# Experts of a routed feed-forward layer: the tile list walked in two halves instead of straight through

## The reference

```python
logits = flat @ router_weight.T + router_bias          # flat: layernorm(x), 4096 x 512
scores = jax.nn.softmax(logits, axis=-1)
topk_vals, topk_idx = jax.lax.top_k(scores, 2)
w = jnp.zeros((T, E)).at[arange(T)[:, None], topk_idx].set(topk_vals)
gu = jnp.einsum('th,ehf->tef', flat, gate_up_proj) + gate_up_bias
gate = jnp.minimum(gu[..., :I], 7.0)
up = jnp.clip(gu[..., I:], -7.0, 7.0)
act = (up + 1.0) * gate * jax.nn.sigmoid(gate * 1.702)
down = jnp.einsum('tei,eih->teh', act, down_proj) + down_bias
out = jnp.einsum('teh,te->th', down, w)
x = x + out
```

## Time and profile before

| | us |
|---|---|
| median of 3 runs | 1872.41 (1872.25 to 1873.85) |
| the profiled execution | 1873.76 |
| its span | 1872.0 |
| mean granted TensorE clock | 0.957 |
| attention and routing, up to the first gate-up matmul | 1130.5 |
| steps 1 to 36 of the expert stage | 671.5 |
| the last two steps and the end | 57.9 |

### The profile page before, as it was taken

The page is one execution under the profiler, slowest core; times in us unless marked ns, Lnnn a source line. Parts: engine busy times, 40 slices in busy tenths (PEclk is TensorE's granted clock), DMA queues, the critical chain, the costliest instruction groups (busy, mean ns, idle before and its releaser), DMA issues. The chain is left out here.

```text
span 1872.0 us, 31059 instructions
## 1 busy us (share of the span) xinstructions
PE 1692.8 (90%) x10405; PEld 1247.7 (67%) x10405; DVE 1334.0 (71%) x2330; ACT 691.5 (37%) x1317; POOL 469.3 (25%) x643
## 2 busy tenths in 40 slices
PE   4799999999999989999998729999999999999996
PEld 4555565555555555555554218998998989889895
DVE  4577667675766676767555587788888888888864
ACT  2254353443533533434334204242434433434221
POOL 3112112121121121121210202434343334233322
PEclk8999999999999999999998859999999999999998
DMA  5333233341332333413212142354544636636322
GB/s 185 86 91 112 85 90 86 94 113 52 112 104 61 100 106 103 112 53 102 75 57 79 46 145 74 106 201 127 191 142 176 218 111 218 212 120 221 96 75 79
DMA packets 104565, 216.04 MB, mean 115 GB/s; under 512 B 26704, under 2 KB 27728, under 8 KB 104400
## 3 DMA queue, kind: packets, MB, share of 16 engines
q1 hardware_dynamic: 77488, 135.53, 22.9%
q0 software_dynamic: 26912, 78.47, 13.3%
HBM read 204.19 MB, written 37.36 MB: 129 GB/s over the span
## 5 line engine op out<-in xcount | busy, mean ns | idle before, releaser
L595 DVE TENSOR_REDUCE negmax<-max_ps 128x2 f32<-128x1024 f32 x256 | 311.6, 1217 | 150.5 <-PE max_ps L376 148.9
L480 ACT ACTIVATE pt<-work 128x512 f32<-128x512 f32 x512 | 278.0, 597 | 327.4 <-PE work L388 325.5
L1188 PE MATMUL gu_ps<-xgT_hi,wg_hi 128*128 128x256 f32 x1248 | 354.8, 284 | 0.0
L1188 PE MATMUL gu_ps<-xgT_hi,wg_lo 128*128 128x256 f32 x1248 | 351.5, 282 | 0.0
L1188 PE MATMUL gu_ps<-xgT_lo,wg_hi 128*128 128x256 f32 x1248 | 351.4, 282 | 0.0
L376 PE MATMUL max_ps<-ks,qs 96*128 96x512 f32 x512 | 190.4, 454 | 56.9 <-DVE negmax L595 39.6
L1188 PEld LDWEIGHTS gu_ps<-xgT_hi,wg_hi 128*128 128x128 f32 x1248 | 235.3, 189 | 0.0
L1188 PEld LDWEIGHTS gu_ps<-xgT_lo,wg_hi 128*128 128x128 f32 x1248 | 235.3, 189 | 0.0
L1188 PEld LDWEIGHTS gu_ps<-xgT_hi,wg_lo 128*128 128x128 f32 x1248 | 235.2, 188 | 0.0
L376 PEld LDWEIGHTS max_ps<-ks,qs 96*128 96x128 f32 x512 | 85.2, 196 | 139.6 <-issue 74.1
L1248 ACT ACTIVATE sig<-gate 128x256 f32<-128x256 f32 x156 | 65.1, 417 | 304.2 <-DVE gate L1300 302.1
(11 more groups left out here) (192 smaller groups left out, 3078.6 us busy)
## 6 DMA issues: line engine op xcount, KB each, us to landing
raw_g<-w_gate_up SPq DMA_DIRECT2D x39, 2048.0 KB
raw_d<-w_down SPq DMA_DIRECT2D x39, 1024.0 KB
ks<-k_hi SPq DMA_DIRECT2D x256, 64.0 KB, 2.1
qs<-q_hi SPq DMA_DIRECT2D x256, 64.0 KB, 2.7
bd<-b_down SPq DMA_DIRECT2D x39, 256.0 KB
x_in<-x SPq DMA_DIRECT2D x8, 1024.0 KB, 5.8
ctxT_raw<-ctx_t SPq DMA_DIRECT2D x8, 1024.0 KB, 6.5
ks<-k_lo POOLq DMA_DIRECT2D x128, 64.0 KB, 2.3
```

Of the source, the lines that this page charges most:

```text
L480: e.activation(pt[k % 2][:, h, :], in_work("exp", u, k, h)[:, :], ACT.Exp, scale=scale).then_inc(exped.sem, 1)
L595: e.tensor_reduce(negmax[:, u % 2, n:n + 2], max_ps[:, :, :], AX.X, ALU.max, negate=True).then_inc(maxed.sem, 1)
L1188: ins = e.matmul(gu_ps[n % GU_BANKS][:, part, :], wg[s][pw][:, k, cols], xgT[s][px][:, k, :], start=(k == 0 and m == 0), stop=(k == KD - 1 ...
```

## The change

A function `in_list` turns a step number into a place of the list: step i takes place i // 2, plus 20 (half of 39, rounded up) for odd i. So even steps walk places 0 to 19 and odd steps places 20 to 38. Each read of the list by a step goes through it: the expert and the flag for a load, the flag for the conversions, the expert's column for the weights of the sum, and the row numbers. The flag of a place now compares it with the place directly before it, which is what its buffer held, and the flag of place 20, the first odd step's, is set to 1. The list itself is made as before.

```diff
+def in_list(i, n_tiles):
+    return i // 2 + i % 2 * ((n_tiles + 1) // 2)
...
-            then(e.memset(changed_f[:, 0:2], 1.0))
-            then(e.tensor_tensor(changed_f[:, 2:], expert_f[:, 2:], expert_f[:, :-2], ALU.not_equal))
+            then(e.memset(changed_f[:, 0:1], 1.0))
+            then(e.tensor_tensor(changed_f[:, 1:], expert_f[:, 1:], expert_f[:, :-1], ALU.not_equal))
+            last()
+            half = in_list(1, n_tiles)
+            then(e.memset(changed_f[:, half:half + 1], 1.0))
...
-    expert = e.value_load(tile_expert[0:1, tile:tile + 1], min_val=0, max_val=experts - 1)
-    changed = e.value_load(tile_changed[0:1, tile:tile + 1], min_val=0, max_val=1)
+    place = in_list(tile, tile_expert.shape[1])
+    expert = e.value_load(tile_expert[0:1, place:place + 1], min_val=0, max_val=experts - 1)
+    changed = e.value_load(tile_changed[0:1, place:place + 1], min_val=0, max_val=1)
...
         def changed_flag(e, i):
-            return e.to_reg(e.value_load(tile_changed[0:1, i:i + 1], min_val=0, max_val=1))
+            place = in_list(i, n_tiles)
+            return e.to_reg(e.value_load(tile_changed[0:1, place:place + 1], min_val=0, max_val=1))
...
-                e.tensor_tensor(w_all[:, :, :], xg[i % 2][:, :, D:DX], tile_hot[:, i, :, :], ALU.mult).then_inc(w_made.sem, 1)
+                e.tensor_tensor(w_all[:, :, :], xg[i % 2][:, :, D:DX], tile_hot[:, in_list(i, n_tiles), :, :], ALU.mult).then_inc(w_made.sem, 1)
...
-                e.tensor_copy(idx[i % IDX][:, :], token_of[:, i * SUB:(i + 1) * SUB]).then_inc(idx_made.sem, 1)
+                place = in_list(i, n_tiles)
+                e.tensor_copy(idx[i % IDX][:, :], token_of[:, place * SUB:(place + 1) * SUB]).then_inc(idx_made.sem, 1)
```

## The result

| | us |
|---|---|
| changed kernel, median | 1850.13 (1844.86 to 1853.42, 4 runs) |
| kernel before, beside it | 1872.33 (1869.89 to 1873.85, 4 runs) |
| ratio | 0.9872, 95% interval 0.9847 to 0.9897 |
| profiled execution and its span | 1853.42, 1851.7 |

Faster by 1.3%, as forecast in sign and inside the range; 3.4 us above the forecast of 1846.7. The profiled execution is 5.4 us above the span that was forecast for it, 1846.3. Where these lie can be read by comparing stages.

What follows compares the result with a forecast made beforehand. TensorE was taken as the bound, with 29.1 us of surplus in eleven steps where it waits for VectorE sums. Saving 25.2, plus 0.2 for routing, minus 0.7 at the end, gave a 25.7 us gain: 1846.7, range 1842.5 to 1856.

Steps and rivals of the forecast that it cites:

- The list read out of the conversions: Expert stage: tiles that change expert, read from weight conversion counts; 6 would change instead of 14, L1148's successor having 32 pieces.
- A quiet step of 17.85 us: Expert stage: a step without waits keeps 17.85 us; every step from 3 to 36 except 24, save tenths in 13 and 16.
- The pair: Neighbouring changing tiles 24 and 25: down and gate-up conversions meet in step 24, costing 2.7 us, bounds 0 and 4.6.
- The single changes: Five tiles changing expert without a changing neighbour: 0 us for steps 10, 23 and 33, at most 0.9 each.
- steps 13 and 16: Steps two behind a single change's down conversion: 0.3 us together from carried VectorE backlog, between 0 and 0.9 each.
- step 31: Kernel before, two steps behind a down conversion: its sum started 1.45 us later than step 11's, with 0.9 us surplus.
- Step 2: Start of the expert stage: its 0.9 us surplus belongs to tiles 0 and 1, which load in both orders, and stays.
- Routing: Where the flags are made: one more VectorE memset on the path, +0.2 us, bounds 0.1 and 0.6.
- The end: Last two sums, waiting for scattered rows to land: 0.7 us less with tile 36 full, bounds -0.7 and +2.
- Every change costs: Rival: each place of change costs 4.0 us, alone or in a pair, giving 1867.9 us; chance 0.06.
- Nothing moves: Rival: the surplus is TensorE's own or loads do not fall, so the time is 1872.6 us; chance 0.05.
- Slower: the clock: Rival: a long dense TensorE stretch in the expert stage lowers its clock to 0.95, giving 1880.5 us; chance 0.03.

Runs made afterwards that it cites:

- the repeat: The changed kernel run again with no edit, beside the kernel before: median 1847.69 us, ratio 0.9871.
- the rotation: Changed kernel with even steps starting at place 17 and wrapping round, so no two changes are neighbours: median 1844.16 us, ratio 0.9845 to the kernel before.
- three more singles: Changed kernel with flags also set at places 3, 10 and 15, so steps 6, 20 and 30 reload and convert alone: steps 3 to 36 took 609.40 us.

## Why the prediction held, and where it didn't

**The list read out of the conversions** was right: 14, 24, 34 and 11, 17, 25 change, L1157 ran 32 times, and the loads' queue moved 27.3 MB less.

**A quiet step of 17.85 us, untouched by the order**: right, in 33 of the 34 steps.

**The pair**: 2.7 forecast, 2.63 measured, as steps 7 and 12 had shown. The mechanism read from the chain, four `wd_hi` ahead of the first sigmoid, is shown by moving them: 1.8 us. That it was the whole of the pair's price I had not claimed, and it isn't.

**The single changes**: 0 forecast, and 0 measured, for the five in the change and for three more. The 0.3 us kept for steps 13 and 16 did not come. The reading of step 31, a backlog that needs time to drain, agrees with the 1.1 us where no quiet step lies between and with the 0.4 us in step 23 behind a pair.

**Step 2**: I said that its 0.9 us stays. It went in the profile, but the time came back ahead of it: from the row list to step 3 the stretch is 0.4 us longer. The first 96 gate-up matmuls took 13.35 us at a mean clock of 0.84, against 12.09 at 0.94. Rows of TensorE (us, busy, granted clock, DMA share, GB/s) after and, second, before:

```profile
1135.02:1148.37 13.35, 13.35 (x98) 0.84 0.23 68
```

```profile
1130.50:1142.59 12.09, 12.09 (x98) 0.94 0.17 48
```

With TensorE later, VectorE had more time for the first two conversions, and step 2 did not wait. The ten profiles in which tile 2 doesn't convert agree: where those matmuls took 12.1 to 12.3 us (three profiles, clock 0.92 to 0.94) step 2 took 18.3 to 19.1, and where they took 13.1 to 13.5 (seven, clock 0.84 to 0.86) it took 17.8 to 18.0. The step that failed is "it stays": the sum of the start is the steadier quantity, not this surplus; the stretch from the row list to step 3 was 60.5 to 62.1 us in these ten.

**Routing**: 0.2 forecast, 0.11 in the first profile and 0.13 in the repeat. The spacing was read too wide: between the two pieces of the earlier trace rows stand two others, the comparison and a memset, and not one.

**The end**: the term with the wrong sign. GpSimd's wait for tile 36's rows did fall, from 2.74 us to 2.02:

```profile
1825.18 0.99 POOL L1432 DMA_INDIRECT acc<-out,idx  x1 [2.02 <-DMA out<-acc,idx]
```

But I had looked at one of five landings. The chain of work that ended last shows the gathers of the sums for tiles 37 and 38 in the changed kernel:

```profile
1826.47 3.94 DMA acc<-out,idx
...
1838.43 4.20 DMA acc<-out,idx
```

and before, where both tiles are spare ones:

```profile
1847.71 3.69 DMA acc<-out,idx
...
1859.41 3.70 DMA acc<-out,idx
```

0.25 and 0.50 us more, and the last scatter took 0.15 longer, from its issue to the end: +0.2 in all and not -0.7. In the other profiles of the expert stage's changed order the end was 57.8 to 58.4 us where nothing else was moved, so the term is nothing that can be told from 0.

**What the sum left out** is the largest: 4.5 us of the attention stage in the profiled execution, 3.8 of them an input load that landed late. I took everything ahead of the routing stage as fixed, and named it a sign of a wrong forecast if the span before the first gate-up matmul moved by more than 0.6 us. It moved by 4.5 (1130.50 to 1135.02), and in the repeat by 2.0 the other way; over all profiles it is 1125.4 to 1135.4. So that sign came in, but it tests the executions and not the change. Against the repeat, whose attention stage was short, the same sum errs the other way: span 1844.8 against the 1846.3 forecast.

**The rivals.** "Every change costs" would have given 1867.9; three more changes for 0.0 us refute it. "Nothing moves" fell: the most occupied engine was left as it was and the kernel is 1.3% faster, because that engine's waits were made by work of the other two. The Trainium skill ("Perfetto Trace Analysis", section "Identifying the Most-Contended Engine") says to optimize the most-contended engine first; that work taken from the others brings nothing was the prediction's own step. The same section judges TensorE's headroom by its matmul rate and its share of weight loads and not by matmul busy time, and that share is 67% here, below VectorE's 71%. "Slower: the clock": the clock was 1.00 over 357 us without a stop, and over 607 us with the rotation. The Trainium skill's statement that activity releases the throttled state ("TensorE: Matmul & The Clock Gate", section "Part 1: The HAM clock gate") agrees with that. The falls to 0.92 all lie in steps that held a stop, but a stop didn't always bring one: step 24 had its 2.6 us at 1.00.

## What to carry to other kernels

Cut the busiest engine's timeline into its repeating steps, subtract a quiet one from each, and ask what the long ones hold: here eleven of 36 steps held 29 us, and all of it came from work on two engines that are busy for 71% and 37% of the span. When such extra work is rare, spread it: the same conversions cost 2.6 us when two met in a step, 1.1 when they followed each other, and nothing when single ones had a quiet step between. And before forecasting a sum to a few microseconds, ask how much the parts that the change doesn't touch vary between executions.

## What the runs showed of the hardware

The attention stage, identical in all kernels, ended between 1066.3 and 1075.5 us in twelve profiles, while steps 3 to 36 repeat to 0.01 us where the clock doesn't fall (609.40 and 609.41 for the changed kernel, 609.40 with three more singles). A load of 1 MB issued at 50 us took 6.1 to 7.3 us to land in nine profiles and 9.3 to 10.3 in three, for no reason that was found.

The page's line of bytes read from memory is no measure of loads that a condition turns off. The loads' queue moved 135.53 MB in the kernel before, 108.24 in the changed one and 91.49 without weight loads from the third tile on, and the line says the same in each. The changed kernel's:

```profile
HBM read 204.19 MB, written 37.36 MB: 130 GB/s over the span
```
